# Sixteen-head attention loop: results turned in the shift's chunk, sums copied before the third unit's exps, lowest parts made by GpSimd

## The reference

```
qkv = einsum('bse,ef->bsf', x, w_qkv)          # x: layer-normed, [2, 1024, 128]
q, k, v = heads of 8 channels, 16 heads
scores = einsum('bhsd,bhtd->bhst', q, k) / sqrt(8)
attn = softmax(scores, axis=-1)
out = einsum('bhst,bhtd->bhsd', attn, v)
return out (heads joined) @ w_out
```

## Time and profile before

| | us |
|---|---|
| median of 3 runs | 1245.65 (1245.39, 1245.65, 1250.24) |
| profiled execution, its own time | 1244.83 |
| its span in the profile | 1243.0 |
| mean granted TensorE clock | 0.939 of full speed |
| busy: PE, DVE, ACT, POOL | 1095.5, 920.2, 711.2, 377.5 |

### The profile page before, as it was taken

The page is one execution under the profiler, slowest core; times in us unless marked ns, Lnnn a source line. Parts: engine busy times, 40 slices in busy tenths (PEclk is TensorE's granted clock), DMA queues, the critical chain, the costliest instruction groups (busy, mean ns, idle before and its releaser), DMA issues. The chain is left out here.

```text
span 1243.0 us, 18745 instructions
## 1 busy us (share of the span) xinstructions
PE 1095.5 (88%) x6921; PEld 555.0 (45%) x6921; DVE 920.2 (74%) x1606; ACT 711.2 (57%) x1207; POOL 377.5 (30%) x239
## 2 busy tenths in 40 slices
PE   4389859999999999999789999999998769999995
PEld 3256745444444444444232222222222267888884
DVE  7958487766666766662789999999997276778777
ACT  5224546433343554434247878777778637888883
POOL 1037311866767666658200000000000021112110
PEclk9569979999999999999659999999999968999998
DMA  4000010000000000010010000000000024233311
GB/s 92 1 1 2 2 34 2 10 1 1 1 2 2 2 1 6 22 44 10 29 64 15 26 14 27 14 26 15 14 2 1 2 35 90 41 77 66 86 35 34
DMA packets 46354, 29.43 MB, mean 24 GB/s; under 512 B 10992, under 2 KB 43000, under 8 KB 46264
## 3 DMA queue, kind: packets, MB, share of 16 engines
q1 hardware_dynamic: 46264, 28.24, 9.8%
HBM read 23.57 MB, written 4.26 MB: 22 GB/s over the span
## 5 line engine op out<-in xcount | busy, mean ns | idle before, releaser
L2034 DVE TENSOR_REDUCE narrow_att_maxima<-psum 128x1 f32<-128x1024 f32 x256 | 301.5, 1218 | 29.1 <-PE psum L1886 26.5
L1993 ACT ACTIVATE narrow_att_probs<-psum 128x512 f32<-128x512 f32 x512 | 266.4, 604 | 79.5 <-PE psum L1912 79.4
L1326 POOL TENSOR_TENSOR gated_tally<-gated_probs,gated_tally 128x1024 f32<-128x1024 f32 x96 | 230.0, 2396 | 62.1 <-ACT gated_probs L1569 53.5
L1569 ACT ACTIVATE gated_probs<-psum 128x1024 f32<-128x1024 f32 x128 | 124.1, 1021 | 188.1 <-PE psum L1459 182.0
L1673 DVE TENSOR_REDUCE gated_maxima<-psum 128x1 f32<-128x512 f32 x256 | 164.5, 684 | 62.4 <-PE psum L1354 60.5
L1912 PE MATMUL psum<-narrow_att_q,narrow_att_k 50*128 50x512 bf16 x448 | 145.4, 383 | 6.3 <-ACT narrow_att_probs L1993 5.2
L1925 PE MATMUL psum<-narrow_att_probs,narrow_att_v_ones 128*32 128x512 f32 x1024 | 137.2, 608 | 10.3 <-ACT narrow_att_sums L1983 10.2
L1886 PE MATMUL psum<-narrow_att_k,narrow_att_q 48*128 48x512 bf16 x448 | 130.3, 381 | 16.2 <-DVE narrow_att_maxima L2034 11.7
L2326 DVE TENSOR_TENSOR moe_hidden_lo<-moe_hidden,moe_hidden_hi 128x512 fp32r<-128x512 f32 x144 | 101.6, 731 | 46.6 <-ACT moe_hidden_hi L2295 46.3
L1472 PE MATMUL psum<-gated_probs,gated_values 128*64 128x512 f32 x512 | 134.0, 612 | 0.0
L2291 ACT ACTIVATE moe_hidden<-psum,moe_up_bias 128x512 f32<-128x512 f32 x144 | 96.0, 685 | 36.9 <-PE psum L73 35.8
(11 more groups left out here) (362 smaller groups left out, 1791.1 us busy)
## 6 DMA issues: line engine op xcount, KB each, us to landing
moe_mixb<-moe_mix_scratch SPq DMA_DIRECT2D x8, 1024.0 KB, 15.8
moe_raw_up<-in_L_ffn_up_w SPq DMA_DIRECT2D x8, 256.0 KB, 16.2
moe_raw_down<-in_L_ffn_down_w SPq DMA_DIRECT2D x8, 256.0 KB, 12.2
narrow_parts_scratch<-gated_values SPq DMA_DIRECT2D x12, 128.0 KB, 2.1
narrow_parts_scratch<-narrow_att_part SPq DMA_DIRECT2D x12, 128.0 KB, 2.1
narrow_att_q<-narrow_parts_scratch SPq DMA_DIRECT2D x14, 96.0 KB
narrow_att_q<-narrow_parts_scratch SPq DMA_DIRECT2D x42, 32.0 KB
narrow_att_k<-narrow_parts_scratch SPq DMA_DIRECT2D x14, 96.0 KB
```

Source lines behind the costliest of these rows:

```text
L1326: pool.tensor_tensor(tally[:, n % 2, :, :], probs[:, kt % 4, :, :], so_far, ALU.add).then_inc(tallied, 1)
L1569: act.activation(probs[:, k % 4, :, :], psum[:, 2 * e:2 * e + 2, :], ACT.Exp, scale=SCALE).then_inc(exped, 1)
L1993: act.activation(probs[:, k % 3, 2 * e + u % 2, :], psum[:, SCORE_BANK + j % 3, :], ACT.Exp, scale=SCALE).then_inc(exped, 1)
L2034: dve.tensor_reduce(maxima[:, n % 2, column(u):column(u) + 1], chunk.rearrange("p a b -> p (a b)"), AX.X, ALU.max).then_inc(chunk_used, 1)
```

## The change

Four things are changed.

1. **Results in the shift's chunk.** The `out` chunks of half groups 0 to 13 are gone. Their work is done within the chunk of shift n+2: PE turns the sums into the chunk's second bank (4 transposes) and then the shift into its first; DVE copies the shift, then takes the reciprocal and multiplies. In time the results of half group n move from unit 5 to unit 11 of half group n+1. `out` 14 stays in unit 5 of half group 15 and `out` 15 is still the tail.
2. **Semaphores of that chunk.** The shift's copy signals SP directly (`shift_copied`); the multiply signals a new semaphore `attended_ready`; DVE waits for both and then signals `chunk_used` by an instruction of its own. The reciprocal no longer waits for the reduce before it. The copy of the sums of half group n waits for the chunk that turned those of n-2 (`turned_with`).
3. **Copy of the sums.** `evacuate(n - 1)` stands ahead of the exps of unit 2.
4. **Lowest parts.** The four `lowest` of the lead run on POOL, behind the filling of `v_ones` for groups 0 and 1, in place of DVE.

```diff
-    def lowest(self, dve, k, part, rest):
-        dve.wait_ge(self.mid_taken, k + 1)
+    def lowest(self, engine, k, part, rest):
+        engine.wait_ge(self.mid_taken, k + 1)
...
-            for n in range(1, HALVES):
-                plan[n * UNITS + 5].append(("out", n - 1))
+            plan[(HALVES - 1) * UNITS + 5].append(("out", HALVES - 2))
...
+            def result_of(c):
+
+                return c[1] if c[0] == "out" else c[1] - 2
+
+            def turned_with(n):
+                return number[("shift", n + 2) if n + 2 < HALVES else ("out", n)]
...
                 for g in range(GROUPS):
+                    if g == 2:
+                        for k in range(2 * PERB, 2 * QUARTERS):
+                            front.lowest(pool, k, part, rest)
...
                 def turn_back(c):
                     i = number[c]
+                    n = result_of(c)
                     pe.wait_ge(chunk_used, i - 1)
+                    if n >= 0:
+                        pe.wait_ge(sums_copied, n + 1)
+                        for i2 in range(QT):
+                            last = pe.transpose(psum[:, i % 2 * 2 + 1, tile(i2)], sums[:, n % 2, tile(i2)], C["ident"])
                     if c[0] == "shift":
                         pe.wait_ge(shift_ready, c[1] + 1)
                         last = pe.transpose(psum[:, i % 2 * 2, :].bitcast(BF16)[0:2 * UNITS, 0:P], shift[:, :], C["ident_bf"])
-                    else:
-                        pe.wait_ge(sums_copied, c[1] + 1)
-                        for i2 in range(QT):
-                            last = pe.transpose(psum[:, i % 2 * 2, tile(i2)], sums[:, c[1] % 2, tile(i2)], C["ident"])
                     last.then_inc(chunk_done, 1)
...
                     if n >= 2:
-                        act.wait_ge(chunk_done, number[("out", n - 2)] + 1)
+                        act.wait_ge(chunk_done, turned_with(n - 2) + 1)
...
                     for u in range(UNITS):
+                        if u == 2 and n >= 1:
+                            evacuate(n - 1)
                         for e in range(2):
...
-                        if u == 2 and n >= 1:
-                            evacuate(n - 1)
...
-                    if u in LOWEST_AT:
-                        front.lowest(dve, LOWEST_AT[u], part, rest)
...
-                        dve.tensor_copy(shift_t[:, :], chunk[:, 0, :].bitcast(BF16)[0:2 * UNITS, 0:P]).then_inc(chunk_used, 1)
-                        dve.wait_ge(chunk_used, i + 1)
-                        dve.sem_inc(shift_copied, 1)
-                    else:
-                        n = c[1]
-                        view = chunk[:, 0, :].rearrange("p (t j d) -> p t j d", t=QT, j=G)
-                        dve.wait_ge(chunk_used, i)
+                        dve.tensor_copy(shift_t[:, :], chunk[:, 0, :].bitcast(BF16)[0:2 * UNITS, 0:P]).then_inc(shift_copied, 1)
+                    n = result_of(c)
+                    if n >= 0:
+                        view = chunk[:, 1, :].rearrange("p (t j d) -> p t j d", t=QT, j=G)
                         dve.reciprocal(inv[:, :].rearrange("p (t j) -> p t j", j=G), view[:, :, :, DH]).then_inc(inv_ready, 1)
                         dve.wait_ge(inv_ready, n + 1)
...
-                                          ALU.mult).then_inc(chunk_used, 1)
+                                          ALU.mult).then_inc(attended_ready, 1)
+                        dve.wait_ge(attended_ready, n + 1)
+                    if c[0] == "shift":
+                        dve.wait_ge(shift_copied, c[1] + 1)
+                    dve.sem_inc(chunk_used, 1)
```

More of the change, by code:

```diff
@@ L1082, in middle @@
         act.activation(part[:, k % 2, 1, quarter(k // 2 % self.PERB)], rest[:, k % 2, :], ACT.Copy).then_inc(self.mid_taken, 1)
-    def lowest(self, dve, k, part, rest):
-        dve.wait_ge(self.mid_taken, k + 1)
+    def lowest(self, engine, k, part, rest):
+        engine.wait_ge(self.mid_taken, k + 1)
         cols = quarter(k // 2 % self.PERB)
-        dve.tensor_tensor(part[:, k % 2, 2, cols], rest[:, k % 2, :], part[:, k % 2, 1, cols],
+        engine.tensor_tensor(part[:, k % 2, 2, cols], rest[:, k % 2, :], part[:, k % 2, 1, cols],
                           ALU.subtract).then_inc(self.low_taken, 1)
@@ L1826, in narrow_attention_phase @@
             CENTER_AT, TURNED_AT = 1, {6: 2, 7: 3}
-            REST_AT, LOWEST_AT = {9: 4, 10: 5, 12: 6, 13: 7}, {11: 4, 12: 5, 14: 6, 15: 7}
+            REST_AT = {9: 4, 10: 5, 12: 6, 13: 7}
             @block.sync
@@ L2039, in _ @@
                             front_behind(u)
-                    elif c[0] == "shift":
+                        continue
+                    if c[0] == "shift":
                         n = c[1]
```

2 lines of the change are left out of this document (1 added, 1 removed).

## The result

| | before | changed |
|---|---|---|
| median of 6 runs, us | 1248.83 (1245.39 to 1250.24) | 1230.46 (1229.28 to 1234.51) |
| profiled execution (span) | 1244.83 (1243.0) | 1231.38 (1229.6) |
| first reduce of the lead to the last reciprocal | 383.08 | 365.96 |
| period of a half group | 21.53 | 20.32 |

The ratio of the two sets of runs is 0.9865, with a 95% interval of 0.9848 to 0.9882, clear of 1: faster by some 17 us; the medians themselves differ by 18.4. The measured median lies in the range, and the forecast of 1228.0 was 2.5 too low. The base moved too: the forecast took 17.6 off a start set by three runs with a median of 1245.65, and six runs of the kernel before have 1248.83.

The account below looks back on a forecast made before the run. The prediction took a chain over PE and ACT, with DVE close behind, to bound the loop. Savings of 8.6 + 8.4 + 0.6 = 17.6 us gave 1227.2 for the profiled execution and a forecast of 1228.0, range 1225.0 to 1233.5.

Parts of the forecast that it names:

- What bounds the kernel: Attention loop: PE and ACT set the ordinary pair of 2.40 us; three longer pairs add 2.34 per half group.
- the chain: Ordinary pair over PE and ACT: score to exp 0.43, released score 0.65, mix 0.32, next score 1.00, together 2.40 us.
- DVE sets the pace: Rival, all pairs of the loop: DVE sets the pace, only the lowest parts' 0.6 is gained, 1245.0 us; chance 0.04.
- Part 1: Unit 5: four transposes of 0.66 us leave the chain in thirteen half groups, 8.6 us off.
- The shift at 0: Shift's pair: PE's new work lies in its wait for DVE, costing 0, bounds 0 and 0.2 us per half group.
- Part 2: Signals of the shift's chunk: the shift's DMA and the copy of the sums keep ample lead, 0 us.
- Part 3: Unit 2: copy of the sums ahead of the exps brings the mix 0.56 earlier in fifteen half groups, 8.4 us off.
- Part 4: Lead: only the fourth lowest part, at 634.45, counts; moved to POOL it takes 0.6 us off, bounds 0.6 and -0.6.
- The sum: Whole kernel: 8.6 + 8.4 + 0.6 = 17.6 us off the profiled 1244.83, giving 1227.2; median forecast 1228.0.
- The clock: Rival, near the experts' start: a longer stretch at half clock makes the kernel slower, some 1252 us; chance 0.02.
- the merged chunk (1236.6): Rival, at the shift: DVE's late reduce delays PE by up to 0.66 per half group, losing 8.6 us; chance 0.08.
- the copy (1234.2): Rival, unit 2: the copy's whole 0.60 lies on the chain, so moving it gives only 2.2 us; chance 0.07.

Follow-up runs that it names:

- last kernel: Changed kernel with the shift's split on POOL and each mix halved by columns (256 of 512 queries per piece, a half group's last mix whole): 1212.66 us, ratio 0.9711.
- mix ahead: Changed kernel with the mix of an odd unit issued ahead of that unit's second score: 1235.23 us, ratio 0.9905, period 20.64.
- split on POOL: Changed kernel with the shift's split done by POOL in three small operations in place of DVE's two: 1228.62 us, ratio 0.985, period 20.25.
- both: Changed kernel with the odd unit's mix ahead of its second score and the shift's split moved to POOL: 1232.59 us, ratio 0.9875, period 20.63.
- heads halved and split on POOL: Changed kernel with each mix cut in two by heads and the shift's split moved to POOL: 1297.51 us, ratio 1.0382, period 24.60.
- lowest parts alone: Kernel before with only the lead's four lowest parts moved to POOL: 1247.55 us in a single execution, period 21.53.
- parts 1 and 2: Changed kernel with the copy of the sums and the lowest parts put back as before: 1238.6 us, ratio 0.9915, period 20.87.
- part 3: Kernel before with only the copy of the sums moved ahead of unit 2's exps: 1240.3 us, ratio 0.9928, period 20.97.
- multiply twice: Changed kernel with DVE's multiply of the results done twice in the shift's chunk: 1234.11 us in a single execution, period 20.57.
- half the reduce: Changed kernel with each reduce of the maxima over 512 of the 1024 keys only: 1223.96 us in a single execution, period 20.21.
- heads halved: Changed kernel with each mix cut in two by heads, 0 and 2 in one unit, 1 and 3 in the next: 1297.16 us, ratio 1.0374, period 24.60.

## Why the prediction was right

**What bounds the kernel** (PE and ACT in the ordinary pair, DVE only at the shift) held: with half of DVE's work gone the pair was 2.40 still. One reading in it was loose. I took eight reduces in 9.55 for DVE's own speed, 2.39 per pair, "close behind the chain". A row that joins eight instructions takes in the short waits between them. Back to back, they stand 1.13 apart in the last kernel (ten in 11.40), 2.26 per pair; the 2.39 was the pace of PE. DVE had 0.14 per pair in hand, so the chance for "DVE sets the pace" could have been lower.

**Part 1**, 13 x 0.66 = 8.6: the half groups lost 0.66 each (period 20.87 alone), and the inner stretch 8.44.

**The shift at 0**, with 0.2 as the bound: the pair is 3.33. DVE's next reduce starts 0.79 behind PE's start (721.07 to 721.86), where I had 0.83; the held maximum starts 0.76 behind it (0.86 by my working), its second half 0.99 (1.11), and the score 1.08, as before. So 0.09 was left where my working had the two within 0.03 of each other. The fit was nearly as tight as the text said: 0.29 more on DVE gave 0.25 more per half group. One half group in the loop is an exception, 20.66 in place of 20.32:

```profile
881.67 1.06 PE L1936 MATMUL psum<-narrow_att_probs,narrow_att_v_ones 128*32 128x512 f32 x8
...
882.82 0.66 PE L1909 MATMUL psum<-ident,narrow_att_sums 128*128 128x128 f32 x4
...
885.36 1.06 PE L1936 MATMUL psum<-narrow_att_probs,narrow_att_v_ones 128*32 128x512 f32 x8
```

The transposes stand 1.15 behind the mix in place of 0.99, and the pair is 3.69. The changed kernel's other profiled execution shows it in the same half group (mixes at 877.71 and 881.39). Both engines are late there: PE's transposes by 0.16, and DVE's reduce behind the split as well (it starts at 881.54, 0.13 ahead of the mix, where the one at 718.67 is 0.47 ahead of 719.14). It costs 0.35 once; its cause stays open.

**Part 2** at 0: no new wait shows for the signals.

**Part 3**, 15 x 0.56 = 8.4: the pair went from 3.15 to 2.59, each link within 0.02, and the part alone gave 8.08.

**Part 4** at 0.6, bounds 0.6 and -0.6: 0.61 in the lead, 0.66 in the inner stretch alone. POOL takes 1.16 for each (1.28 estimated from the earlier trace rows), and DVE's reduce beside the first is 1.22 as elsewhere. The Trainium skill ("Perfetto Trace Analysis", Optimizing Scalar/DVE Operations) has that a move between these two engines, which share a read port of SBUF, might not help; the lead's 0.61 disagrees, here, where DVE's operations in that stretch read PSUM.

**The sum**, 17.6: the inner stretch measured 17.1. The 0.5 that is missing is within the terms, 0.35 of it the odd half group. The profiled execution would then be 1227.7; it took 1231.4, since 3.7 were added outside. That the medians differ by 18.4, and so by more than the inner stretch, is the spread of the executions and not a gain of the change. **The clock**: the stretch behind the loop, that rival's place, took 2.2 longer, within the "few us" that the range had for it; the last section shows how far the clock accounts for it. **The rivals** of the merged chunk (1236.6) and of the copy (1234.2) each would have left a pair longer than 3.34 or 2.59, and none is but the odd one.

## What to carry to other kernels

Where several engines are busy for over 90%, follow one period and write the distance of each pair of landmarks; the sum of what exceeds the ordinary one is what order alone can give. Then find the ring that sets the ordinary one (here score, exp, released score, mix, with three banks) by its links' lags: work in it is shortened, not moved, and an edit beside it changes nothing. Work put into a wait costs nothing up to the wait's end and all of it beyond: measure the margin by doubling the work before adding more, and read an engine's own speed from a stretch in which nobody holds it up.

## What the runs showed that I had not expected

**The same code behind the loop takes 255.0 to 260.7 us**, from the last reciprocal to the end. Windows of the first 50 us in the kernel before:

```profile
988.30:1038.30 50.00, 37.23 (x178) 32.35 (x179) 36.14 (x103) 21.15 (x37) 7.76 (x10) 0.69 0.20 35
```

and of the kernel with the columns halved:

```profile
953.50:1003.50 50.00, 37.45 (x154) 34.11 (x155) 33.48 (x98) 16.73 (x29) 7.72 (x10) 0.56 0.15 25
```

For the changed kernel the row stands further up. The granted clock there was 0.69, 0.66 (changed) and 0.56 (columns halved), and the whole stretch took 255.3, 257.5 and 260.7. The levels are 1.2 and 2.4 GHz, so these means are shares of the two. This stretch gave back 2.2 us of the changed kernel's gain and 5.4 of the last one's.

Over the fourteen profiles the two go together, with one exception:

| granted clock in the first 50 us | profiles | last reciprocal to the end, us |
|---|---|---|
| 0.69 | before; mix ahead; split on POOL; both; heads halved and split on POOL | 255.0 to 255.7 |
| 0.69 | lowest parts alone | 257.6 |
| 0.66 | changed (two); parts 1 and 2; part 3; multiply twice; half the reduce; heads halved | 256.6 to 258.0 |
| 0.56 | columns halved | 260.7 |

So more of the 50 us at 1.2 GHz goes with a longer stretch, but the second row is 2.3 longer than the kernel before at the same clock: the clock isn't all of it. A busier loop isn't the cause by itself: with only the lowest parts moved, the loop is that of before, and with the mix ahead or the split on POOL, at some 95 of 100 for PE, the stretch took 255.0 and 255.7; with the heads halved, at 99.13 of 100, the clock was 0.66 and 0.69. The prediction argued for an unchanged clock from fewer gaps in the loop, by the Trainium skill ("TensorE: Matmul & The Clock Gate", Part 1), which has the gate follow how busy PE has been; these rows neither follow that argument nor give a rule in its place. What decides stays open. The kernel before differs in the same way with itself: of its 43 executions whose clock is on record, 36 took 1245.3 to 1250.7 at a mean granted clock of 0.932 to 0.939, and seven took 1254.9 to 1256.2 at 0.927 or 0.928. None of the seven was profiled, so where they lost their time isn't shown.

**The lead's start differs by 4.3 us between executions** with the same code ahead of it: the first reduce stands at 602.54 to 606.82 in the fourteen profiles. Differences of a few us between two single executions of this kernel are therefore no evidence on the loop, and this is why the readings above go by the inner stretch and by periods.

**Matmuls on fewer groups of 32 rows aren't shorter**: 0.98 for two heads against 0.99 for four, and 0.58 for half of the columns.
